# A graph network on one core: how VectorE makes the one-hots of the source tiles in layers 1 and 3

## The reference

```python
x = _layernorm(x + _L0(x, edge_attr, ...))
x = _layernorm(x + _L1(x, edge_index, W, b))
x = _layernorm(x + _L2(x, edge_index, edge_type, ...))
x = _layernorm(x + _L3(x, edge_index, edge_weight, ...))
# layer 1
aggregated = segment_sum(x[src], dst) / max(degree, 1)
out = relu((aggregated + x) @ W.T + b)
# layer 3
x = node_features @ W
msg = x[row] * norm[:, None]
out = segment_sum(msg, col) + b
```

## Time and profile before

| | |
|---|---|
| median of 3 runs | 3749.47 us (3747.87 to 3751.64) |
| the profiled execution | 3743.15 us, span of its instructions 3741.4 us |
| mean granted TensorE clock in it | 0.964 |
| PE busy | 2820.6 us, 75% of the span |
| VectorE busy | 2495.4 us, 67% |
| GpSimd busy | 1847.8 us, 49% |
| ScalarE busy | 1517.8 us, 41% |
| line 1891, VectorE | 516 instructions, 0.69 us each |
| gather of layer 1 | about 1466 to 1810 us of the span |
| gather of layer 2 | about 2183 to 2710 us |
| gather of layer 3 | about 3078 to 3425 us |

### The profile page before, as it was taken

The page is one execution under the profiler, slowest core; times in us unless marked ns, Lnnn a source line. Parts: engine busy times, 40 slices in busy tenths (PEclk is TensorE's granted clock), DMA queues, the critical chain, the costliest instruction groups (busy, mean ns, idle before and its releaser), DMA issues.

```text
span 3741.4 us, 94994 instructions
## 1 busy us (share of the span) xinstructions
PE 2820.6 (75%) x23282; PEld 2453.3 (66%) x23283; DVE 2495.4 (67%) x7099; ACT 1517.8 (41%) x4312; POOL 1847.8 (49%) x2243
## 2 busy tenths in 40 slices
PE   8555544444439986887799689999999958887996
PEld 6232322222229975777799479999899957776995
DVE  7666666666647778555577777777666777554667
ACT  0111100000004445555577543222365348886765
POOL 4777777777763341777433354444521007774000
PEclk9999999999999997999899899999999989998998
DMA  6444444444448943778698035555378807885883
GB/s 216 150 150 141 149 143 146 147 143 149 141 131 285 292 144 104 279 274 280 216 293 274 9 115 175 177 179 183 126 241 248 263 30 273 272 283 194 289 286 123
DMA packets 419041, 721.75 MB, mean 193 GB/s; under 512 B 68624, under 2 KB 198169, under 8 KB 417932
## 3 DMA queue, kind: packets, MB, share of 16 engines
q1 hardware_dynamic: 330492, 494.35, 42.7%
q0 software_dynamic: 88464, 226.43, 16.1%
HBM read 481.26 MB, written 285.09 MB: 205 GB/s over the span
## 4 chain that ended last, share of the span: by engine, by line
PE 42%; POOL 23%; issue 13%; DMA 11%; DVE 5%; ACT 3%; SPq 2%; DVEq 2%; POOLq 1%; ACTq 0%
PE ps L1375 20%; POOL slots L750 19%; PE ps L1408 9%; DMA gbuf<-ring_raw,to_blk 8%; PE ps L1410 5%; POOL gbuf L804 3%; DMA ring_raw<-gbuf 2%; PE ps L1420 2%; PE ps L1250 2%; PE ps L1461 1%; DVEq L501 1%; PE ps L1452 1%; DVE stats L1935 1%; SPq L501 1%; ACT ring_raw L976 1%
## 5 line engine op out<-in xcount | busy, mean ns | idle before, releaser
L804 POOL DMA_INDIRECT gbuf<-ring_raw,to_blk x774 | 754.4, 975 | 727.4 <-DVE ring_raw L1868 257.9
L750 POOL DMA_INDIRECT slots<-ring_raw,idx_edges x782 | 751.4, 961 | 242.2 <-issue 242.2
L1375 PE MATMUL ps<-ring_raw,memory 128*128 128x128 f32 (+2 forms) x6576 | 784.6, 279 | 82.6 <-DVE memory L1836 49.2
L1375 PEld LDWEIGHTS ps<-ring_raw,memory 128*128 128x128 f32 x6576 | 764.5, 193 | 104.9 <-issue 56.3
L1836 DVE TENSOR_TENSOR memory<-dst_lane,lane_ids 128x512 f32<-128x512 f32 x774 | 535.1, 692 | 74.8 <-POOL dst_lane L768 51.7
L1286 PE MATMUL ps<-memory 128*49 128x343 bf16 (+6 forms) x784 | 263.5, 489 | 387.9 <-DVE memory L1732 386.6
L1408 PE MATMUL ps<-memory 128*128 x2752 | 497.8, 273 | 9.9 <-DVE memory L1877 7.5
L1846 DVE TENSOR_TENSOR memory<-memory,ps 128x128 f32 (+2 forms) x1032 | 294.6, 285 | 308.3 <-PE ps L1375 294.8
L935 ACT ACTIVATE memory<-lane_ids,dst_lane 128x128 f32<-128x128 f32 x1032 | 330.3, 392 | 403.2 <-PE ps L1375 246.1
L1410 PE MATMUL ps<-memory 128*128 x2752 | 477.4, 220 | 0.0
L1286 PEld LDWEIGHTS ps<-memory 128*49 128x49 bf16 x784 | 113.9, 159 | 530.4 <-DVE memory L1732 301.6
(11 more groups left out here) (283 smaller groups left out, 4781.6 us busy)
## 6 DMA issues: line engine op xcount, KB each, us to landing
ring_raw<-gbuf SPq DMA_DIRECT2D x669, 268.0 KB, 3.6
ring_raw<-in_edge_attr SPq DMA_DIRECT2D x111, 448.0 KB, 3.8
ring_raw<-slots SPq DMA_DIRECT2D x153, 272.0 KB, 4.1
zr<-lane_rows SPq DMA_DIRECT2D x87, 384.0 KB
zt<-lane_rows SPq DMA_DIRECT2D x87, 384.0 KB
memory<-lane_rows SPq DMA_DIRECT2D x84, 384.0 KB, 4.8
memory<-slots SPq DMA_DIRECT2D x105, 272.0 KB, 4.1
memory<-gbuf SPq DMA_DIRECT2D x105, 268.0 KB, 3.8
```

Source lines behind the costliest of these rows:

```text
L750: pool.indirect_dma_start(edges, bass.IndirectOffsetOnAxis(idx_edges[0:n, u, j:j + 1], 0), edge_rows[0:n, u, j, :], None).then_inc(scatter ...
L804: pool.indirect_dma_start(gbuf, bass.IndirectOffsetOnAxis(to_blk[:, t:t + 1], 0), node_rows[:, r, :], None, bounds_check=NBLK - 1, oob_is_ ...
L1375: ins = pe.matmul(bank(r % 3, width), hots[:, r, j * P:(j + 1) * P], rows[:, j, 0:width], start=j == 0, stop=j == BLK - 1)
```

## The change

In `one_hots`, used in layers 1 and 3 alone, the `tensor_tensor` of the lanes with the spread PSUM column becomes a `tensor_scalar` of the lanes with a scalar per partition, read from `row_t[:, 1:2]` in SBUF. The values compared and the output (f32, 128x512) are the same. The copy of line 1897 that filled the PSUM column, and the wait for it, go; the PSUM column is no longer used. No semaphore, no DMA and no order of instructions changes on any engine: 516 instructions are of another kind, and two are gone.

```diff
-        row_shown = ps[:, 7, 511:512]
 ...
                         dve.wait_ge(gathered, i * RING + (base + r + 1))
-                        dve.tensor_tensor(hots[:, r, :], (lane_odd if odd else lane_bc)[r // LANE_SETS][:, r % LANE_SETS, :],
-                                          row_shown.broadcast_to([P, BLK * P]), ALU.is_equal).then_inc(src_hots, 1)
+                        dve.tensor_scalar(hots[:, r, :], (lane_odd if odd else lane_bc)[r // LANE_SETS][:, r % LANE_SETS, :],
+                                          row_t[:, 1:2], None, ALU.is_equal).then_inc(src_hots, 1)
                         if beside is not None:
                             beside(i - 2, r)
 
-                if layer != 2:
-                    link(dve.tensor_copy(row_shown, row_t[:, 1:2]))
                 if layer == 2:
```

## The result

The changed kernel takes 3761.73 us (median of 9 runs, 3754.78 to 3767.40); the kernel before, on the same chip, 3747.87 us (9 runs, 3744.77 to 3754.14). The ratio is 1.0034 with a 95% interval from 1.0024 to 1.0045: **slower by 0.34%**, 14 us between the medians, 9 to 17 by the interval. The profiled run of after took 3759.08 us with a span of 3757.3.

A forecast was written before the change was run, and what follows sets the result against it. GpSimd's indirect DMAs were taken to bound both gathers. Shorter one-hots (0), the dropped copy (0) and delayed DMAs (11 us), added to the 3749.47 us median, gave 3760 us; the forecast's own range was 3753 to 3771, at 50%.

The forecast's parts named there:

- The bound: Gathers of layers 1 and 3: GpSimd's indirect DMAs bind; any faster engine can bring 19.7 us at most.
- Part 1: VectorE's one-hots in both gathers: 0.689 us each becomes 0.474 us, worth nothing because GpSimd's pitch hides it.
- Part 2: Before the first one-hot of layers 1 and 3: dropping the copy and its wait gains 0, at most 1.3 us together.
- Part 3: Both gathers: the new one-hots delay 19% of GpSimd's indirect DMAs by 0.122 us on average, 12.0 us in all.
- The need at 0.12 us: GpSimd's indirect DMA, 0.12 us after its start, needs something a one-hot begun some 0.11 us ahead holds until it ends.
- the 21 us at 0.03: Both gathers: if one-hots starting as late as 0.03 us before a DMA still delay it, the sum is 21.2 us.
- The even spread of positions: Both gathers: every position of VectorE's starts against GpSimd's DMAs was taken as equally likely, giving 19% of tiles delayed.
- what other waits absorb: Layer 3's gather: part of the delay vanishes in the 12.5 us GpSimd waits anyway, say 1 us.
- A: Rival for both gathers: the new one-hots don't delay the DMAs, so 3749.5 us, within 3745 to 3755; chance 33%.
- B: Rival for both gathers: any one-hot running at a DMA's start makes it wait, 45 us more, 3795 us; chance 11%.
- C: Rival for both gathers: shorter one-hots remove some of the 19.7 us, most in layer 3's start; 3742 us; chance 6%.
- What would show it: Trace of layers 1 and 3: some hundred of 516 DMAs above 1.00 us, mean near 1.00, step 1.30 us.

The follow-up runs named there:

- the column in SBUF: The kernel before, still a tensor_tensor, with the column spread over the 512 elements in SBUF instead of PSUM and no copy; ratio to before 1.0159, +63.6 us.
- the halves: The changed kernel with each compare cut into two tensor_scalars of 256 elements, back to back; ratio to the kernel before 1.0024, +9.5 us.
- the kernel with a running sum: The changed kernel with its tensor_scalar also writing a running sum of its result to a spare SBUF column; ratio to the kernel before 1.0007, +3.3 us.
- the strided form: The changed kernel with the same tensor_scalar walking the 512 elements as 128 groups of 4, each 128 apart; ratio to the kernel before 1.0223, +81.7 us.
- the three tiles at once: The changed kernel with one tensor_scalar of 1536 elements for three tiles instead of three of 512; ratio to the kernel before 1.0150, +55.9 us.

## Why the prediction was right, step by step

**The bound.** GpSimd's indirect DMAs bound both gathers, as said. One-hots of 0.49, 0.69, 0.70, 0.75 and 0.80 us, and of 1.76 us for three tiles, were run: the time follows the DMAs' length in all of them and VectorE's in none. 0.75 us that don't hold cost -2.5 and +3.3 us; 0.49 us that hold cost 13.9.

**Part 1, the length.** Forecast 0.474 us, worth nothing. The median is 0.490; 110 of the 516 took over 0.59 because they were held in turn. Worth nothing is borne out.

**Part 2, the copy.** Worth nothing too. In after TensorE's first matmul comes 1.62 us after ScalarE's last normalisation in layer 1, the same 1.62 as before, and 1.55 us after VectorE's last instruction of line 2197 (2200 before) in layer 3, where it was 1.64: 0.09 us at most.

**Part 3, the hold.** This term carried the forecast: 98 tiles (19% of 516) by 0.122 us, 12.0 us. Measured at this moment of the DMA: 98 tiles, 11.9 us. The need at 0.12 us is 0.13 (the delay is the one-hot's end less 0.13), and the latest start that still counts is some 0.09 to 0.10 us ahead, where I had 0.11. Of the rows that gave the law, only line 1972's is a tensor_scalar; lines 1732 and 1836 are tensor_tensors of two SBUF inputs, a kind that the rule quoted beside them does not name and that counts from later starts too (0.05 us ahead with the column in SBUF, 0.03 for line 1836's fourth), so the 21 us at 0.03 did not apply. That both figures meet the forecast so closely is in part luck. The even spread of positions, which I could not test, did not hold: 35 one-hots begin 0.25 to 0.20 us ahead of a DMA and 10 begin 0.15 to 0.10 ahead, where an even spread has 19 in each; with it, and the measured 0.49, 0.13 and 0.095, the same working gives some 14 us and not 11.9. In the halves and with the column in SBUF the spread is not even either. Missing from the sum was the second moment (23 DMAs, 1.4 us). Too small was what other waits absorb: I took 1 us off, it was 3.5. These two errors work against each other: +11 was forecast and 9.5 are in the gathers of the profile, 13.9 between the medians. Single profiles and medians differ by as much as these 4 us in the kernel with a running sum too (3.3 and -0.7), so which of the two is nearer is not shown.

**The rivals.** A (no delay) tied it to one-hots of 0.755 us or to starts in step; the one-hots ran at 0.49 and the starts hit as often as chance has it. The form that A described is the one with the running sum: 0.748 us, DMAs at 0.976. B (whoever overlaps the start waits, +45) fell: DMAs with a one-hot over their start that had begun less than 0.09 us ahead took their 0.97. The rule of the Trainium skill by its letter ("SBUF — State Buffer", "Who interferes with whom": the pair is held for the whole instruction, and the second comer waits) gives B; by the trace the DMA waits only if the one-hot began early enough and still runs at 0.13 or 0.85 us of a DMA that lasts 0.97. C (faster) fell: 0.2 us less per one-hot won nothing that shows. GpSimd's pauses in layer 3 did shrink by 3 us, but longer DMAs alone do that: with the column in SBUF, whose one-hots are as long as before, the pauses of both gathers fell from 173.8 to 161.1 us.

**What would show it.** 116 DMAs of the two layers are above 1.00 us (a hundred were said; 7 in before), their mean is 1.00, layer 2's stayed at 0.974. The step from start to start is 1.328 in layer 1 and 1.336 in layer 3, where I gave 1.30. That number was wrong by its own working: before's mean steps are already 1.301 and 1.325, and the hold adds 0.026 and 0.011.

What stays open: which side, reading or writing, of what they share the DMA needs at 0.13 and at 0.85 us. The runs show when a DMA is late, not what it wants. Why the strided form takes 0.80 us is open as well.

## What to carry to other kernels

Where GpSimd's indirect DMAs bound a stage, choose VectorE's instructions there by whether they hold GpSimd and not by their length: here 0.75 us that leave it alone cost nothing, and 0.49 us that hold it cost 14 us. Keep one operand of 512 elements in PSUM, or take the form with an accumulator; if an instruction must hold, make it short, since the loss grows faster than its length (+14 us at 0.49 us per tile, +56 at 1.02 us per three tiles). Before costing such an edit, look for rows where the bounding engine's instruction is longer than its median, and see what the others ran at its start: a handful of such rows gave this forecast.

## What the runs showed that I had not expected

- An indirect DMA of 0.97 us has a second moment: a one-hot of 0.49 us that begins 0.38 to 0.46 us after its start delays it by the one-hot's end less 0.85 us (23 DMAs, up to 0.10 us each). With the three tiles at once it cost 24 us.
- VectorE is held as well: a one-hot that begins 0.46 to 0.74 us after an undisturbed DMA's start ends 1.23 us after it, up to 0.77 us long in place of 0.49. So is one that begins just ahead of the DMA: 16 that began 0.09 to 0.04 us ahead all end 0.46 us after its start, the longest 0.55 us long. It costs nothing here, since VectorE has time.
- The column in SBUF in place of PSUM costs 63.6 us with the same instruction at the same length, partly because a held DMA brings the next one into step with a one-hot that holds it again.
- A tensor_scalar keeps its hold on GpSimd when its order of elements makes it slow (0.80 us, +81.7 us).
